# Six expert slots filled from the first nine tiles of rows and put through the first chunk during the last routing and the gather

## The reference

```python
x = layernorm(x + attention(x))     # 16 heads of 32, causal, position bias (alibi), Wq Wk Wv Wo with biases
logits = x @ Wr + br                # 4 experts
probs = softmax(logits); top_w, top_idx = top_k(probs, 1)
g = x @ Wg[e]; u = x @ Wu[e]        # 512 -> 2048, for the one expert e of each token
y = (silu(g) * u) @ Wd[e]           # 2048 -> 512
x = layernorm(x + y * top_w)
```

## Time and profile before

| | before |
|---|---|
| median of 3 runs | 1234.6 us |
| profiled execution: its own time | 1232.5 us |
| profiled execution: span, first to last instruction | 1230.7 us |
| mean granted TensorE clock | 0.966 |
| busy in the span: PE | 1141.4 us |
| busy: DVE, ACT, POOL | 729.8, 587.7, 520.5 us |

### The profile page before, as it was taken

One profiled execution on the slowest core, in us unless ns is written; L12 is line 12 of the kernel. 1 busy time (PEld: TensorE's weight loads), 2 busy tenths in 40 slices (PEclk: granted clock), 3 DMA queues, 4 the chain that ended last, 5 costly groups with the idle time before them and its releaser, 6 DMA issues.

```text
span 1230.7 us, 25807 instructions
## 1 busy us (share of the span) xinstructions
PE 1141.4 (93%) x7658; PEld 1021.8 (83%) x7658; DVE 729.8 (59%) x1975; ACT 587.7 (48%) x1475; POOL 520.5 (42%) x662
## 2 busy tenths in 40 slices
PE   6898999999999975799999999999999999999994
PEld 5687877887888754799889989989988998998893
DVE  4565677667666745464664665466366555546664
ACT  3587877876887663342323233233233323323343
POOL 6866665755676563531330231133033113113336
PEclk9999999999999886799999999999999999999997
DMA  9223333233322221442222323213221331321202
GB/s 289 53 64 72 74 86 87 53 80 105 80 66 61 70 78 68 144 123 70 61 78 70 90 56 86 80 52 86 70 83 56 87 87 44 91 73 60 80 36 103
DMA packets 105374, 100.10 MB, mean 81 GB/s; under 512 B 10271, under 2 KB 79519, under 8 KB 105248
## 3 DMA queue, kind: packets, MB, share of 16 engines
q1 hardware_dynamic: 100064, 87.18, 26.3%
q0 software_dynamic: 3040, 9.18, 2.3%
q10 hardware_dynamic: 2144, 2.10, 0.6%
HBM read 64.74 MB, written 9.18 MB: 60 GB/s over the span
## 4 chain that ended last, share of the span: by engine, by line
PE 49%; POOL 7%; DMA 3%; issue 2%; ACT 2%; DVE 1%; SPq 0%; POOLq 0%; ACTq 0%; DVEq 0%
PE bank L921 36%; PE bank L946 7%; POOL up_lo L1652 6%; DMA up_raw<-in_Wu_dram 3%; PE bank L933 3%; ACT up_hi L1076 1%; PE bank L693 1%; PE bank L895 1%; PE bank L787 1%; POOL out_dram L1719 1%; PE bank L883 0%; DMA y<-x_scratch,row_token 0%; SPq L617 0%; DVE oT_lo L1263 0%; POOL y_rstd L1712 0%
## 5 line engine op out<-in xcount | busy, mean ns | idle before, releaser
L1652 POOL TENSOR_TENSOR up_lo<-up_raw,up_hi 128x256 fp32r<-128x256 f32 x241 | 171.7, 747 | 487.7 <-ACT up_hi L1076 487.6
L921 PE MATMUL bank<-up_hi,xsT_hi 128*128 x1216 | 356.6, 293 | 9.7 <-POOL up_lo L1652 8.2
L921 PE MATMUL bank<-up_hi,xsT_lo 128*128 x1216 | 345.0, 284 | 0.0
L921 PE MATMUL bank<-up_lo,xsT_hi 128*128 x1216 | 344.9, 284 | 0.0
L1467 DVE SCALAR_TENSOR_TENSOR h_tok<-bank,row_weight,silu 128x128 f32<-128x128 f32 x304 | 93.4, 347 | 296.7 <-ACT silu L1161 296.7
L1643 POOL TENSOR_TENSOR pT_lo<-probs,pT_hi 128x512 fp32r<-128x512 f32 (+1 forms) x192 | 211.2, 1107 | 128.1 <-ACT pT_hi L1053 127.2
L921 PEld LDWEIGHTS bank<-up_hi,xsT_hi 128*128 128x128 f32 x1216 | 233.7, 192 | 16.4 <-issue 16.1
L1161 ACT ACTIVATE silu<-bank 128x256 f32<-128x256 f32 (+1 forms) x160 | 59.9, 374 | 368.2 <-PE bank L921 368.2
L921 PEld LDWEIGHTS bank<-up_hi,xsT_lo 128*128 128x128 f32 x1216 | 234.4, 193 | 0.3
L921 PEld LDWEIGHTS bank<-up_lo,xsT_hi 128*128 128x128 f32 x1216 | 234.0, 192 | 0.0
L1484 DVE TENSOR_TENSOR y<-bank,y 128x512 f32<-128x512 f32 x295 | 199.0, 690 | 0.4
(11 more groups left out here) (181 smaller groups left out, 2075.7 us busy)
## 6 DMA issues: line engine op xcount, KB each, us to landing
stack<-qk SPq DMA_DIRECT2D x180, 128.0 KB, 2.4
up_raw<-in_Wg_dram SPq DMA_DIRECT2D x64, 256.0 KB, 3.7
up_raw<-in_Wu_dram SPq DMA_DIRECT2D x64, 256.0 KB, 4.1
down_raw<-in_Wd_dram SPq DMA_DIRECT2D x64, 256.0 KB, 2.6
x_tok<-in_x_dram SPq DMA_DIRECT2D x16, 256.0 KB, 3.4
x_scratch<-res SPq DMA_DIRECT2D x12, 256.0 KB, 2.3
w_raw<-in_Wo_dram SPq DMA_DIRECT2D x1, 1024.0 KB, 8.7
stack<-max_row SPq DMA_DIRECT2D x64, 2.0 KB
```

The lines of the kernel that those rows point to most:

```text
L921: mm = pe.matmul(bank[:, n * 2 * P:(n + 1) * 2 * P], a[:, s, k, :], up_w[w][k][:, :, :].rearrange("p a f -> p (a f)")[:, bass.ds(at, 2 * P ...
L1652: pool.tensor_tensor(up_w[1][k][:, e, :], up_raw[:, idx % NUPS, k, :, :].rearrange("p g f -> p (g f)"), up_w[0][k][:, e, :].bitcast(F32), ...
```

## The change

From the first nine tiles of rows (ET = EARLY + NE - 1) at least six whole tiles of 128 rows of one expert can be formed. These become slots 0 to 5 (EARLY). Their routing is done inside the attention loop as `route_ahead`, 31 small DVE steps in eleven parts at steps that the planner gives, with two side jobs on PE: EC (ten matmuls: ranks and counts) and EL (nine: the list). Part 6 waits at least for step XT_FREE = U - 12. Six gathers (`gather_ahead`) stand in POOL's queue at six successive steps from GATHER = U + 2 on, each behind that step's `unit_low`. Six side jobs EX turn the gathered tiles, after the loop, ahead of OP of tile 15. The full routing at the end covers the rest in slots 6 to 18: its positions take the early slots into account with six more DVE steps.

PE's order after the last logit becomes: the two counting matmuls, up_pair(0, 0), the listing, up_pair(0, 1), transpose 0, up_pair(0, 2), transposes 1 and 2, three down slots (EDOWN), and then chunk 0's other slots. The four down splits of chunk 0 stand in DVE's queue between `lane_hot` and `row_token`, and row_weight and the first gate_pair right behind it. `y`, `xsT_hi` and `xsT_lo` become single tiles so that the early slots' can lie where attention has already left its memory, and the second x1T buffer lies over `xT_hi`, so ACT no longer waits there for the last scores (`s_sT`).

The core of the diff:

```diff
+EARLY = 6
+ET = EARLY + NE - 1
+EPAIR = EARLY // 2
+EDOWN = 3
+A_HOT, A_PLACED, A_SLOT = 5, 28, 31
...
-R_DIFF, R_HOT, R_COUNT, R_PLACE, R_LANE = 3, 6, 11, 27, 28
+R_DIFF, R_HOT, R_COUNT, R_PLACE, R_LANE = 3, 6, 11, 33, 34
...
+            "EC": [53] * (ET + 1), "EL": [53] * ET, "EX": [53] * 4}[kind]
...
+XT_FREE, GATHER = U - 12, U + 2
...
     def rank(u, half, job):
         g = min(u // PER_GROUP, NG - 1)
+        if job[0] in ("EC", "EL") or g // GPB == LAST and job == (job[0], ET - 1):
+            return 0
...
+        for after, parts in ((("logit", ET - 1), range(0, 2)), (("EC", 0), range(2, 10)), (("EL", 0), range(10, 11))):
+            if plan.flushed.get(after) == u:
+                at = u + 1
+                for part in parts:
+                    if part == 6:
+                        at = max(at, XT_FREE)
+                    plan.ahead_at[at] = part
+                    at += 1
+        if plan.flushed.get(("EL", 0)) == u:
+            for slot in range(EARLY):
+                plan.gather_at[max(u + 1, GATHER) + slot] = slot
...
-    for job in list(queue):
+    for job in [j for j in queue if j != ("OP", NT - 1)] + [("EX", slot) for slot in range(EARLY)] + [("OP", NT - 1)]:
         plan.add(job, 6)
...
@@ tensor, after the tail @@
+            pe.wait_ge(s_ahead, A_SLOT)
+            for s in range(EARLY):
+                registers[s] = pe.alloc_register(f"slot{s}_expert")
+                pe.load(registers[s], a_expert[0:1, s:s + 1])
+            pe.wait_ge(s_route, R_HOT)
+            hot = hot_pad[:, NT - 1:, :].rearrange("p t e -> p (t e)")
+            pe.matmul(routed[:, 0:NT * NE], ones_r[:, :], hot, start=True, stop=True).then_inc(s_counts, 1)
+            pe.matmul(ranks[:, 0:NT * NE], before_r[:, :], hot, start=True, stop=True).then_inc(s_rank, 1)
+            up_pair(0, 0)
+            pe.wait_ge(s_placed, 2)
...
+            mm.then_inc(s_listed, 1)
+            for pr in range(1, EPAIR):
+                up_pair(0, pr)
+                transpose_pair(0, pr - 1)
+            transpose_pair(0, EPAIR - 1)
+            for s in range(EDOWN):
+                down_slot(0, s)
             for c in range(NC - 1):
-                for pr in range(NPAIR):
+                pr0, s0 = (0, 0) if c else (EPAIR, EDOWN)
+                for pr in range(pr0, NPAIR):
...
@@ tensor, split_rows(s) @@
-                if s >= 3:
-                    pe.wait_ge(s_xsTlo, s - 2)
+                if s >= EARLY + 3:
+                    pe.wait_ge(s_xsTlo, s - EARLY - 2)
+                else:
+                    pe.wait_ge(s_y, s % 3 + 1)
...
@@ vector, attention loop @@
+                if u in plan.ahead_at:
+                    route_ahead(plan.ahead_at[u])
@@ vector, route_ahead, part 9 @@
+                    ahead_step(dve.tensor_tensor(lane_hot[:, 0:ET, :], small[:, C_LANE:C_LANE + P].unsqueeze(1).to_broadcast([P, ET, P]),
+                                                 a_lane.unsqueeze(2).to_broadcast([P, ET, P]), ALU.is_equal))
...
@@ vector, routing @@
+            step(dve.tensor_tensor(count, count, a_size[:, :], ALU.subtract))
...
+            step(dve.tensor_tensor(begins, begins, a_rest[:, :], ALU.add))
+            step(dve.tensor_tensor(sooner, a_begins[:, :], begins, ALU.subtract))
...
+            step(dve.tensor_tensor(rt(EQ), rt(POS), a_size[:, :].unsqueeze(1).to_broadcast([P, NT, NE]), ALU.is_lt))
+            step(dve.tensor_tensor(rt(EQ), rt(EQ), sooner.unsqueeze(1).to_broadcast([P, NT, NE]), ALU.mult))
...
+            step(dve.tensor_tensor(rt(POS), rt(POS), rt(EQ), ALU.add))
...
+            for e in range(NE):
+                split_down(0, e)
             dve.wait_ge(s_listed, 1)
             step(dve.tensor_scalar(row_token[:, :], number, -1.0, 0.0, ALU.add, ALU.max))
...
+            gate_pair(0, 0)
...
@@ gpsimd, attention loop @@
             for u in range(STEPS):
                 if LAG < u <= U + LAG:
                     unit_low(u - LAG - 1)
+                if u in plan.gather_at:
+                    gather_ahead(plan.gather_at[u])
```

419 lines of the change are left out of this document (287 added, 132 removed).

## The result

The changed kernel is slower. Measured beside the kernel before it took 1248.6 us (median of 1245.5 to 1252.0) against 1234.8, a ratio of 1.0125 with a 95% interval of 1.0091 to 1.0159. Measured a second time it was 1238.9 against 1233.8: 1.0053, 1.0030 to 1.0076. The two intervals don't overlap, and why isn't known. Both say slower, by about 1.3% and 0.5%. The prediction was 1234.0, no change, 1228 to 1241.

The account below looks back on a forecast made before the run. TensorE was taken to bound the kernel nearly everywhere, except a dip around the routing. 7.5 - 3.4 - 1.5 - 2.0 = 0.6 us gained from 1232.5 gives 1231.9; the runs' median stands 2.1 above, so 1234.0, range 1228 to 1241.

Parts of the forecast that it names:

- Part 8: Inside the attention loop: 31 DVE steps and 19 small matmuls cost 2.0 us, bounds 0 and 10.5.
- The rival that DVE paces the loop: In the attention loop: all 8.5 us of added DVE work count instead of 0.8, giving 1241.7; chance 0.15.
- Part 1: Routing after the last logit: six small DVE instructions ahead of R_PLACE add 1.35 us.
- Part 2: Routing hole: up_pair(0, 0) fits into PE's 7.4 us wait, ends 3.7 us before PE is wanted, costs nothing.
- The rival of an early clock: Routing: up_pair(0, 0) lifts the clock and the listing holds it, giving 1229.5; chance 0.22.
- Parts 3 and 4: Routing to fourth pair: splits delay row_token, early pairs and down slots cover the gather; 7.5 us gained.
- Part 5: Step from chunk 0 to 1: early down slots gain zero, PE waits some 2.2 us; loss up to 2.
- Part 6: Last attention steps: six gathers in POOL's queue delay the last pT_lo, 3.4 us lost, bounds 0 and 6.8.
- the rival of hidden gathers: Last attention steps: POOL's gathers fit into its waits, the 3.4 us fall away, giving 1230.6; chance 0.10.
- Part 7: Behind the loop: six EX jobs ahead of OP 15 make the tail 1.5 us later, bounds 0.2 and 4.0.

Follow-up runs that it names:

- the kernel with the steps alone: Kernel before with tile 8 put ahead of K and Q of group 14, plus the 31 early DVE steps; no EC, EL or gathers: 1.0051 of before.
- the late splits: Changed kernel with POOL's low parts of the first two experts' up weights issued behind the loop: 1.0039 of before.
- the milder order: Changed kernel with only x1t and logit of tile 8 put ahead, budget of the last steps 1000 instead of 700: 1.0078 of before, again 1.0072.
- order alone: Kernel before with the planner putting tile 8 (OT, OP, x1t, logit) ahead of K and Q of group 14: 1.0024 of before.

## Why the prediction was wrong

*Part 8, 31 DVE steps and 19 small matmuls: the step that failed.* It charged 0.8 us for DVE and 1.2 for PE, and nothing for the order of tile 8. Measured: 1.8 to 2.3 for the order, and 7.8 to 9.0 for the steps, of which 4.4 arise without EC and EL; EC and EL by themselves nothing. The 8.5 us of DVE work were sized rightly (8.6). The mistake was to take a busy share of six to seven tenths for room. The work of a head is a chain through PE, DVE, ACT and POOL, and DVE's instructions stand in it in a fixed order, so added steps in front of a mask can delay that unit. The waits of 0.81 and 0.87 us in the kernel with the steps alone fit this; how much of each is due to the steps isn't shown. And part 8 had no term for the clock: it fell where PE had waited, and in the second changed profile it stood at 0.50 for some 5 to 6 us at a time (to 426, 439 and 453) while PE was full for most of it. The earlier trace rows show granted clocks of 8, 8, 6 and 7 in slices 14 to 17 before the change, two of them in the loop; that was the warning. Shorter windows of the kernel before show it at its plainest:
```profile
408.00:412.00 4.00, 2.50 (x13) 1.72 (x13) 3.80 (x12) 2.00 (x6) 1.26 (x1) 0.81 0.19 70
412.00:416.00 4.00, 4.00 (x15) 3.14 (x14) 1.73 (x6) 2.84 (x7) 2.64 (x4) 0.50 0.40 89
```
DVE had next to no room there, PE was idle 1.5 us, and the clock fell. Tile 8's logit came in step 172, not near 165, and the last part of the early routing stands at step 189. The rival that DVE paces the loop named the mechanism and its bound of 8.5; it should have had the largest chance. It added 7.7 us to the forecast; the loop measured 7.4 to 8.9 more than part 8 had. That the two agree so well is in part luck, since the loop's figure holds the order's 1.8 to 2.3 us, for which the rival had nothing.

*Part 1, the routing grows.* From the first routing step to the listing it was 9.6 us before and is 11.2 (508.09 - 496.90, and 11.2 in the first profile): 1.5 against 1.35.

*Part 2, the first pair in the hole.* As predicted; it ends 3.7 us before the listing in the second profile, 4.7 in the first. In the first profile the clock rose at 502.4, 3.1 us into the pair, and had fallen again when the listing came; in the second it didn't rise. By the Trainium skill, "TensorE: Matmul & The Clock Gate", "What's actually happening", sustained activity releases the throttle; the first trace agrees with that here, and in the second the pair's 5.5 us of unbroken matmuls passed without a rise. The rival of an early clock was half right on the rise and wrong on its being held: the listing took 3.62 us in both, as before.

*Parts 3 and 4.* Fourth pair 28.4 us behind the first routing step (predicted 28.8). The clock came back 3.1 us into pair 1 in the second profile, 4.0 in the first, where 4.7 was taken. PE waits 0.90 for h_tok ahead of the last transpose (predicted 1.1). Gain of the stage 7.6 to 7.9 against 7.5. The mechanism and the size hold in the second profile; in the first, 4 us were lost to the late silu, a wait that neither the prediction nor a rival had.

*Part 5.* The wait is 2.05 and 2.21 us (predicted 2.2). The clock fell in it in the first profile, and the stage grew by 1.1 to 1.4 us; in the second neither happened. Both are within the bound of 2.

*Part 6.* 3.1 to 3.6 against 3.4 (its five gathers add up to 6.7, not 6.8). The queue is followed in order, and nothing was hidden: the rival of hidden gathers is refuted, and the late splits show that it was the queue's length. The first gather took 1.28 and 1.29 us, the others 1.01 to 1.04 in the second profile. By the Trainium skill, "SBUF — State Buffer", "Who interferes with whom", a VectorE tensor_scalar or copy between SBUF tiles would have kept GpSimd out. DVE's timeline has no such instruction beside the gathers, as the prediction said, so no run here tests that rule.

*Part 7.* 0.0 to 1.3 against 1.5: the 24 transposes took 4.90 us in the first profile and 3.96 in the second instead of 5.1, and OP 15 ran at the full clock as predicted, where it took 4.18 us before:
```profile
471.39 3.96 PE L863 MATMUL bank<-ident,y 128*128 128x128 f32 x24
475.11 0.48 PE L762 MATMUL bank<-w_hi,oT_hi 128*128 128x512 f32 x1
```

*The sum.* With the second profile's stages in place of the terms: 7.8 - 3.3 - 0.2 - 10.7 + 0.1 = -6.3, where the prediction had +0.6. The other terms together came out 1.8 us better than predicted; part 8 alone is 8.7 us worse.

**Left open.** Why the steps cost 7.8 to 9.0 with EC and EL in the kernel and 4.4 without, while EC and EL alone cost nothing, isn't settled; taking PE's wait for lane_hot away didn't change it. DVE's wait for EC, which the kernel with the steps alone leaves out, isn't the reason either: in the second changed profile DVE took EC's result at 409.0 and began the step that needs it at 412.5, with no idle time just ahead of it. Two more takes on DVE, and each later take one step later in the planner's list, are the candidates, and neither was run by itself. Each price rests on one or two profiled executions, which differ by 1.2 us in the changed loop. Which part of the lower clock is cause and which is result is open too: with the milder order at a clock of 0.94 the loop still lost 7.4 to 7.9. So are the late silu, which isn't the loads but goes with the milder order, and the distance between the two measurements of the changed kernel.

## What to carry to other kernels

An engine that is busy two thirds of the time in a software pipeline need not have a third to give, since others wait in order for what it does; look at windows of a few us before calling it free. Here added work on DVE cost from three tenths of its length (1.4 us for 4.9) to all of it (9.0 for 8.5), and more than half of the larger price was matmuls at the lower TensorE clock. A move that wins 8 us in a hole must be charged with all that has to be ready for it, and here that was prepared on the path that bounds the kernel. Compare traces by stages between fixed events, with two executions of the kernel before at hand: here the loop and the routing of the kernel before repeated within 0.5 us, those of the changed kernel within 1.2 and 4.1, and whole spans of the changed kernel differed by 12.3, more than the change was worth.

## What the runs showed of the hardware

More than half of what the steps cost in the changed kernel's loop was TensorE's clock: 4.4 and 5.8 us of longer busy time for the same matmuls, beside 3.4 and 3.1 us more idle time. Between heads 49 and 62, length and granted clock were:

| kernel | length, us | mean clock | length x missing clock, us | DVE busy, us |
|---|---|---|---|---|
| before | 85.1, 85.6 | 0.96, 0.94 | 3.4, 5.1 | 55.5, 55.4 |
| order alone | 87.4 | 0.96 | 3.5 | 55.8 |
| changed without steps | 87.1 | 0.94 | 5.2 | 55.4 |
| order and steps | 91.8 | 0.93 | 6.4 | 64.4 |
| changed | 94.9, 96.1 | 0.89, 0.88 | 10.4, 11.5 | 63.8, 63.9 |
| a further instruction behind each step | 97.5 | 0.88 | 11.7 | 68.7 |
| without the order of tile 8 | 89.2 | 0.90 | 8.9 | 64.8 |
| milder order, twice | 94.9, 93.0 | 0.91, 0.94 | 8.5, 5.6 | 64.7, 65.6 |

From before to the changed kernel the missing clock goes from 3.4 and 5.1 to 10.4 and 11.5, the length less that from 81.7 and 80.5 to 84.5 and 84.6. With the milder order less of it is clock and more is waiting. (The column overstates the loss where PE was idle anyway, and the means are rounded to 0.01, some 0.4 us.) Not every wait brought a fall: in the first profile of before PE was busy 5.5 of the 8 us from 432 to 440, and the granted clock stayed at 1.00. And a fall wasn't undone by dense work at once: in the kernel with the order and the steps PE was full from 436 to 440, and the granted clock was 0.50 throughout. The rise wasn't the same twice: in the pairs of 24 matmuls without a break it came 3.1 us into pair 0 and 4.0 into pair 1 in the first changed profile, in the second not within pair 0's 5.5 us and 3.1 into pair 1 (ahead of pair 1 stood the 3.6 us of the listing).
